# Reordering the queues of a cross-attention stage: scores behind the query product, normalises in one run, a subtraction ahead of the statistics

## The chip, the cores and the metric

The kernel runs on one core of a Trainium2 chip. Times are device microseconds of one execution. The engines are TensorE (PE, with its weight loads PEld), VectorE (DVE), ScalarE (ACT), GpSimd (POOL) and SyncE (SP), which here only issues transfers.

## The reference, cut to what matters

Six layers run one after the other on x (128 batches of 32 rows of 128). The change touches the first, a cross-attention of 16 heads with 64 features each. Its queries are the layer-normed rows of x ("latents"); its keys and values come from 257 context rows and the 32 latents.

```python
xn, ln_lat = layer_norm(ctx, g1, b1), layer_norm(latents, g2, b2)
q = ln_lat @ Wq
k, v = split(concatenate([xn, ln_lat], axis=1) @ Wkv)
weight = einsum('bhld,bhnd->bhln', q * scale, k * scale)
weight = softmax(where(full_mask, weight, neg), axis=-1)
out = einsum('bhln,bhnd->bhld', weight, v)
return out @ Wout                     # added to x
```

## The kernel before, in words

`xattn0` never forms keys and values. For each head it keeps the 128 x 128 products A (of the query and key weights) and U (of the value and output weights). So the scores are (latents x A) against the normed context rows, and the output is (probabilities x context rows) x U, summed over heads.

The work is cut into 128 batches. Four batches make a tile of 128 query rows, and 32 tiles make x. The 512 rows of a batch (16 heads x 32 rows) are worked on in four groups of 128. Each engine runs a function `step(g, j)` for batch s = 8g + j; the middle of the stage is a hardware loop over g with eight steps written out. Within a step the order of work on each engine is the order in the code, and semaphores order the engines among themselves. Different parts of a step serve different batches: `live(g, j, n)` says that batch s + n exists, so the edges of the stage leave parts out.

In a step for batch s TensorE does, in this order:

- `score` for groups 0 and 1 of batch s + 1 (L812), into two PSUM banks that the groups share by turns
- `turn` of batch s: eight transpositions of the normalised probabilities (L822)
- `score` for groups 2 and 3 of batch s + 1
- `query`: a quarter of the queries of the next tile (L859), into one PSUM bank
- in the first step of a tile (b == 0) the projection of the finished tile with U, 16 products (L881)
- the values of batch s in two halves (L840), and between them the transposition of the tails (L831) and of a context block of batch s + 3 (L893)
- the values of the tail rows (L851), with which the output of the batch is complete.

VectorE masks each group and takes its row extreme (L684), copies the first turned half (L695), takes statistics and normalises context rows for batches s + 4 and s + 5 (L703, L710, L717), forms the reciprocal of the four row sums (L722) and the scaled tail probabilities (L724), subtracts to get the low half of the queries (L731) and of the turned context (L740), and adds the projection to x (L736).

ScalarE takes the exponentials (L755), normalises each group of probabilities with the reciprocal (L760, four instructions a step), and copies out of PSUM: the second turned half (L769), the high half of the queries (L776), the turned tails (L785), the high half of the context (L791), and the output (L796).

A tile's score needs both halves of the queries, the turn of batch s + 1 needs all four normalises of it, and the tail values (L851) need the copy L785. GpSimd applies the affine part of the context norm, and SP loads context rows eight batches ahead, once z of the batch that used the slot is done.

Of the kernel before, what the change touches and what calls it, by code (L numbers as in the profile page):

```python
# [20 lines left out]
ALU = mybir.AluOpType  # L21
# [3 lines left out]
ds = bass.ds  # L25
# [414 lines left out]
def live(g, j, ahead, n=B):  # L440

    return not isinstance(g, int) or 0 <= 8 * g + j + ahead < n
# [93 lines left out]
def xattn0(k, io):  # L536
# [8 lines left out]
    with ExitStack() as stack:  # L545
# [42 lines left out]
        def quarter(b):  # L588


            return (1, b + 1) if b < 3 else (2, 0)
# [6 lines left out]
        with nc.Block() as block:  # L598
# [78 lines left out]
            @block.vector  # L677
            def _(dve):
                def mask(g, j, grp):
                    s, n, par = g * 8 + j, (j + 1) % 8, (j + 1) % 2  # L680
                    if n % 4 == 0 and grp == 0:
                        dve.wait_ge(keys_ready, tile_of(g, j, 1) + 1)
                    wait_apart(k, dve, scored, s * 4 + (5 + grp))
                    nc.vector.tensor_tensor_reduce(  # L684
                        out=neg[:, grp, :], in0=score_ps[grp % 2][:, 0:KEYS0], in1=bias[:, n, :], scale=-DH0 ** -0.5,
                        scalar=3.4e38, op0=ALU.add, op1=ALU.min, accum_out=nmax[:, par, grp:grp + 1]).then_inc(masked, 1)

                def step(g, j):
                    s, t, u, b = g * 8 + j, tile_of(g, j), j // 4, j % 4
                    if live(g, j, 1):  # L690
                        mask(g, j, 0)
                        mask(g, j, 1)
                    if live(g, j, 0):
                        dve.wait_ge(turned[0], s + 1)
                        nc.vector.tensor_copy(probT[:, 0, :], turn_ps[0][:]).then_inc(probT_ready[0], 1)  # L695
                    if live(g, j, 1):
                        mask(g, j, 2)
                        mask(g, j, 3)
                    if live(g, j, 5):
                        n, par = (j + 5) % 8, (j + 5) % 2  # L700
                        dve.wait_ge(raw_loaded[n], (g + (j + 5) // 8 + 1) * 16)
                        for kt in range(2):
                            last = nc.vector.bn_stats(stats[:, par, kt, :], raw[:, n, kt, :])  # L703
                        last.then_inc(stats_ready, 1)
                    if live(g, j, 4):
                        n, par = (j + 4) % 8, j % 2
                        dve.wait_ge(rstd_ready, s + 5)
                        wait(dve, xn_ready, s + 3)
                        for kt in range(2):
                            last = nc.vector.tensor_scalar(z[:, par, kt, :], raw[:, n, kt, :], mv[:, par, kt, 0:1],  # L710
                                                           rstd[:, par, kt:kt + 1], ALU.subtract, ALU.mult)
                        last.then_inc(z_ready, 1)
                    if live(g, j, 5):
                        par = (j + 5) % 2
                        wait_apart(k, dve, stats_ready, s + 6)
                        for kt in range(2):
                            last = nc.vector.bn_aggr(mv[:, par, kt, :], stats[:, par, kt, :])  # L717
                        last.then_inc(mv_ready, 1)
                    if live(g, j, 1):
                        par = (j + 1) % 2  # L720
                        dve.wait_ge(exped, s * 4 + 8)
                        nc.vector.reciprocal(rinv[:, par, :], rsum[:, par, :]).then_inc(rinv_ready, 1)  # L722
                        dve.wait_ge(rinv_ready, s + 2)
                        nc.vector.tensor_tensor(  # L724
                            prob_tail[:, par, :, :, 0:TAIL0].rearrange("p i f n -> p f i n"),
                            prob[:, par, :, 2 * P:KEYS0].rearrange("p (f i) n -> p f i n", f=2),
                            rinv[:, par, :].rearrange("p (f i) -> p f i", f=2).unsqueeze(3).broadcast_to([P, 2, 2, TAIL0]),
                            ALU.mult).then_inc(tail_prob_ready, 1)
                    if live(g, j, 4 * quarter(b)[0] - b):
                        dve.wait_ge(q_hi, (t + quarter(b)[0]) * 4 + (quarter(b)[1] + 1))  # L730
                        nc.vector.tensor_tensor(q_half(g, j, LO), q_ps[:].rearrange("p (h b l) -> p h b l", h=4, l=L),  # L731
                                                q_half(g, j, HI), ALU.subtract).then_inc(q_copied, 1)
                    if b == 0 and live(g, j, -1):
                        dve.wait_ge(proj_ready, t)
                        xt = k.x[:, ds((t - 1) * D, D)]
                        nc.vector.tensor_tensor(xt, proj_ps, xt, ALU.add).then_inc(x_added, 1)  # L736
                    if live(g, j, 3):
                        dve.wait_ge(xnT_hi, s + 4)
                        n = (j + 3) % 8
                        nc.vector.tensor_tensor(xnT[:, LO, n, 0:2 * P], ctx_ps[:, 0:2 * P], xnT[:, HI, n, 0:2 * P],  # L740
                                                ALU.subtract).then_inc(xnT_ready, 1)
                    if b == 0 and live(g, j, -1):
                        wait_apart(k, dve, x_added, t)
                        tile_stats(k, t - 1).then_inc(x_stats_ready, 1)

                dve.wait_ge(zeroed, 1)
                run_steps(dve, step, LEAD, LAG)
                dve.wait_ge(x_stats_ready, TILES)

            @block.scalar  # L750
            def _(act):
# [3 lines left out]
                    nc.scalar.activation(prob[:, par, grp, :], neg[:, grp, :], ACT.Exp, bias=nmax[:, par, grp:grp + 1],  # L755
                                         scale=-1.0, accum_out=rsum[:, par, grp:grp + 1]).then_inc(exped, 1)

                def normalise(g, j, grp):
                    part = prob[:, (j + 1) % 2, grp, 0:2 * P]
                    return nc.scalar.activation(part, part, ACT.Copy, scale=rinv[:, (j + 1) % 2, grp:grp + 1])  # L760

                def step(g, j):
                    s, t, u, b = g * 8 + j, tile_of(g, j), j // 4, j % 4
                    if live(g, j, 1):
# [2 lines left out]
                    if live(g, j, 0):  # L767
                        act.wait_ge(turned[1], s + 1)
                        nc.scalar.activation(probT[:, 1, :], turn_ps[1][:], ACT.Copy).then_inc(probT_ready[1], 1)  # L769
                    if live(g, j, 1):  # L770
                        exp(g, j, 2)
                        exp(g, j, 3)
                    ahead, hg = quarter(b)
                    if live(g, j, 4 * ahead - b):
                        act.wait_ge(q_ready, (t + ahead) * 4 + (hg + 1))
                        nc.scalar.activation(q_half(g, j, HI), q_ps[:].rearrange("p (h b l) -> p h b l", h=4, l=L),  # L776
                                             ACT.Copy).then_inc(q_hi, 1)
                    if live(g, j, 1):
                        act.wait_ge(rinv_ready, s + 2)
                        act.wait_ge(exped, s * 4 + 8)  # L780
                        normalise(g, j, 0)
                        normalise(g, j, 1)
                    if live(g, j, 0):
                        act.wait_ge(turned[2], s + 1)
                        nc.scalar.activation(probT[:, 2, 0:2 * P], turn_ps[0][:, 0:2 * P], ACT.Copy).then_inc(probT_ready[2], 1)  # L785
                    if live(g, j, 1):
                        normalise(g, j, 2)
                        normalise(g, j, 3).then_inc(prob_ready, 1)
                    if live(g, j, 3):
                        act.wait_ge(ctx_turned, s + 4)  # L790
                        nc.scalar.activation(xnT[:, HI, (j + 3) % 8, 0:2 * P], ctx_ps[:, 0:2 * P], ACT.Copy).then_inc(xnT_hi, 1)  # L791
                    if live(g, j, 0):
                        act.wait_ge(out_ready, s + 1)
                        if b == 0:
                            wait(act, proj_ready, t)
                        nc.scalar.activation(oT[:, :, b * L:(b + 1) * L].rearrange("p (f h) l -> p f h l", f=2),  # L796
                                             out_ps[:, :, 0:2 * P].rearrange("p f (h l) -> p f h l", l=L), ACT.Copy).then_inc(oT_ready, 1)
# [4 lines left out]
            def _(pe):  # L802
# [60 lines left out]
                def step(g, j):  # L863
# [5 lines left out]
                    if here:  # L869
                        turn(g, j, 0)  # L870
                        turn(g, j, 1)
                    if ahead:
                        score(g, j, 2)
                        score(g, j, 3)
                    if live(g, j, 4 * quarter(b)[0] - b):
                        query(g, j)
                    if b == 0 and live(g, j, -1):
                        pe.wait_ge(oT_ready, s)
                        wait(pe, xnT_ready, s + 3 if live(g, j, 2) else B)
                        for h in range(H):  # L880
                            last = nc.tensor.matmul(proj_ps, oT[:, h, :], k.U[:, h, :], start=(h == 0), stop=(h == H - 1))  # L881
                        last.then_inc(proj_ready, 1)
                    if here:
                        values(g, j, 0)
                        turn_tails(g, j)
# [1599 lines left out]
```

## Time and profile before

| | |
|---|---|
| median of 3 runs | 2382.99 us (2381.13 to 2385.65) |
| the profiled execution | 2381.13 us, of which its span is 2379.0 us |
| busy share of TensorE / weight loads | 84% / 65% |
| busy share of VectorE / ScalarE / GpSimd | 69% / 68% / 38% |
| granted TensorE clock, mean | 0.917 of full speed |

The stage that the change touches begins some 70 us after the span's start and ends at about 1030 us. A busy share is the time with at least one instruction in progress. TensorE's instructions are pipelined and their ends are modelled, so their starts are the better thing to read. VectorE's and ScalarE's instructions overlap their successors by a few hundredths of a microsecond.

### The profile page before, as it was taken

To read this page: it belongs to the slowest core of one execution; us is meant where nothing else is said; L and a number is where in the kernel's file an instruction comes from. 1 tells how busy PE (TensorE), PEld (TensorE's weight loads), DVE (VectorE), ACT (ScalarE), POOL (GpSimd) and SP (SyncE) were. 2 spreads that over 40 slices of the span, in tenths; PEclk is the share of its full clock that TensorE was granted. 3 is DMA by queue.
4 is the path that set the end of the run, shared out by engine and by line. 5 is a ranking of instruction groups with operands and counts; after the bars stand their busy time and mean duration, and the time that the engine had idled before them with its cause. 6 is when DMAs were issued, how large, how long until landed. Compare 5 with 4: busy or idle time off the path is not lost. (4 is left out here: it accounts for less than half of the span.)

```text
span 2379.0 us, 56007 instructions
## 1 busy us (share of the span) xinstructions
PE 1989.1 (84%) x15622; PEld 1552.4 (65%) x15622; DVE 1637.6 (69%) x5167; ACT 1626.3 (68%) x4429; POOL 907.8 (38%) x1342
## 2 busy tenths in 40 slices
PE   3799999999999999962600579999999989859997
PEld 2688888888888888841500247777777756526665
DVE  5777777777777777638667637787787778854554
ACT  3588888888777888852644358887887878644443
POOL 2533443334433333203145023333333357534554
PEclk8799999999999999985755789999999999969999
DMA  4211111111111111000000022222222100010001
GB/s 132 69 32 32 32 32 32 34 33 33 37 33 31 31 31 31 3 1 0 0 0 0 0 69 65 70 61 64 70 61 64 49 2 0 1 27 1 1 0 35
DMA packets 113673, 77.03 MB, mean 32 GB/s; under 512 B 12385, under 2 KB 99777, under 8 KB 113473
## 3 DMA queue, kind: packets, MB, share of 16 engines
q1 hardware_dynamic: 112086, 73.99, 11.5%
q10 hardware_dynamic: 1194, 1.58, 0.2%
q8 instruction: 34, 0.56, 0.1%
q0 software_dynamic: 320, 0.60, 0.1%
q14 instruction: 39, 0.31, 0.0%
HBM read 71.67 MB, written 4.46 MB: 32 GB/s over the span
## 5 line engine op out<-in xcount | busy, mean ns | idle before, releaser
L755 ACT ACTIVATE a_prob<-a_neg,a_nmax 128x289 f32<-128x289 f32 x512 | 270.4, 529 | 80.5 <-DVE a_nmax L684 75.0
L1646 ACT ACTIVATE b_prob<-b_neg,b_nmax 128x257 f32<-128x257 f32 x512 | 255.6, 505 | 97.6 <-DVE b_nmax L1596 97.5
L650 POOL TENSOR_TENSOR a_xn<-a_z,g 128x256 f32<-128x256 f32 x128 | 93.3, 729 | 525.4 <-DVE a_z L710 525.4
L812 PE MATMUL a_score<-a_xnT,a_qT 128*128 128x290 f32 x1536 | 274.3, 314 | 1.1 <-DVE a_qT L731 1.1
L840 PE MATMUL a_out<-a_probT,a_xn 128*128 128x256 f32 x1024 | 263.5, 380 | 0.3 <-DVE a_probT L695 0.3
L684 DVE CUSTOM_DVE_ANT_0 a_neg<-a_score,a_bias 128x289 f32<-128x289 f32 x512 | 220.9, 459 | 46.9 <-PE a_score L812 40.9
L812 PEld LDWEIGHTS a_score<-a_xnT,a_qT 128*128 128x128 f32 x1536 | 215.9, 190 | 43.8 <-issue 43.2
L760 ACT ACTIVATE a_prob<-a_prob,a_rinv 128x256 f32<-128x256 f32 x512 | 230.2, 498 | 1.0 <-DVE a_rinv L722 1.0
L1596 DVE CUSTOM_DVE_ANT_0 b_neg<-b_score,b_bias 128x257 f32<-128x257 f32 x512 | 195.9, 421 | 31.9 <-PE b_score L1688 31.8
L840 PEld LDWEIGHTS a_out<-a_probT,a_xn 128*128 128x128 f32 x1024 | 174.9, 191 | 13.7 <-DVE a_probT L695 0.6
L740 DVE TENSOR_TENSOR a_xnT<-a_ctx,a_xnT 128x256 fp32r<-128x256 f32 x128 | 54.4, 425 | 160.2 <-ACT a_xnT L791 160.2
L2348 POOL TENSOR_TENSOR m_hidden<-m_full,m_hidden 128x512 fp32r<-128x512 f32 (+1 forms) x88 | 113.9, 1294 | 128.7 <-ACT m_hidden L2329 128.7
L1574 POOL TENSOR_TENSOR b_weight<-own_value,b_rinv 128x128 f32<-128x128 f32 x128 | 51.3, 401 | 262.0 <-DVE b_rinv L1614 261.9
L859 PE MATMUL a_q<-latT,A 128*128 (+1 forms) x1024 | 139.6, 281 | 6.5 <-DVE a_qT L731 4.2
L1693 PE MATMUL b_turn<-ident,b_prob 128*128 128x128 f32 x1024 | 143.3, 281 | 0.0
L1693 PEld LDWEIGHTS b_turn<-ident,b_prob 128*128 128x128 f32 x1024 | 109.1, 141 | 46.3 <-ACT b_prob L1646 42.0
L859 PEld LDWEIGHTS a_q<-latT,A 128*128 128x128 f32 x1024 | 131.2, 197 | 7.9 <-DVE a_qT L731 5.2
L1390 PE MATMUL f_down<-f_up,f_downT 128*128 x48 | 23.3, 638 | 133.4 <-DVE f_up L1362 133.3
L822 PE MATMUL a_turn<-ident,a_prob 128*128 128x128 f32 x1024 | 132.7, 273 | 1.4 <-ACT a_prob L760 1.3
L2324 ACT ACTIVATE m_silu<-m_g 128x512 f32<-128x512 f32 (+1 forms) x88 | 52.6, 598 | 116.5 <-PE m_g L1986 116.5
L881 PE MATMUL a_ctx<-U,a_oT 128*128 128x128 f32 x1024 | 119.7, 275 | 0.7 <-ACT a_oT L796 0.7
L822 PEld LDWEIGHTS a_turn<-ident,a_prob 128*128 128x128 f32 x1024 | 118.8, 141 | 2.0 <-ACT a_prob L760 2.0
(472 smaller groups left out, 5321.1 us busy)
## 6 DMA issues: line engine op xcount, KB each, us to landing
a_raw<-in_ctx SPq DMA_DIRECT2D x128, 128.0 KB, 3.3
b_raw<-in_ctx SPq DMA_DIRECT2D x128, 128.0 KB, 3.2
a_kept<-keep SPq DMA_DIRECT2D x32, 257.0 KB, 3.9
b_kept<-keep SPq DMA_DIRECT2D x32, 257.0 KB, 3.6
b_v_rows<-ctx_tail_values SPq DMA_DIRECT2D x32, 256.0 KB, 3.5
a_tail<-latents_normalised SPq DMA_DIRECT2D x64, 64.0 KB
latents_normalised<-lat_affine SPq DMA_DIRECT2D x8, 256.0 KB, 2.3
out<-x SPq DMA_DIRECT2D x1, 2048.0 KB
```

Source lines behind the costliest of these rows:

```text
L684: nc.vector.tensor_tensor_reduce(out=neg[:, grp, :], in0=score_ps[grp % 2][:, 0:KEYS0], in1=bias[:, n, :], scale=-DH0 ** -0.5, scalar=3.4e ...
L755: nc.scalar.activation(prob[:, par, grp, :], neg[:, grp, :], ACT.Exp, bias=nmax[:, par, grp:grp + 1], scale=-1.0, accum_out=rsum[:, par, g ...
L760: return nc.scalar.activation(part, part, ACT.Copy, scale=rinv[:, (j + 1) % 2, grp:grp + 1])
L812: last = nc.tensor.matmul(score_ps[grp % 2][:, 0:even(KEYS0)], qT[:, a, un, bn, 4 * grp:4 * grp + 4, :], xnT[:, c, n, :], start=(p == 0), ...
L822: last = nc.tensor.transpose(turn_ps[kt][:, grp * P:(grp + 1) * P], prob[:, j % 2, grp, kt * P:(kt + 1) * P], k.ident[:])
L840: nc.tensor.matmul(out_ps[:, half, 0:2 * P], xn[:, j, kt, :], probT[:, kt, half * 2 * P:(half + 1) * 2 * P], start=(kt == 0), stop=False)
L859: last = nc.tensor.matmul(q_ps[:, h * P:(h + 1) * P], k.A[:, 4 * hg + h, :], k.latT[:, ds((t + ahead) * P, P)], start=True, stop=True)
L881: last = nc.tensor.matmul(proj_ps, oT[:, h, :], k.U[:, h, :], start=(h == 0), stop=(h == H - 1))
L1596: nc.vector.tensor_tensor_reduce(out=neg[:, par, grp, :], in0=score_ps[grp][:, 0:N_CTX], in1=bias[:, n, :], scale=-DH1 ** -0.5, scalar=3.4 ...
L1646: nc.scalar.activation(prob[:, n, grp, :], neg[:, par, grp, :], ACT.Exp, bias=nmax[:, par, grp:grp + 1], scale=-1.0, accum_out=rsum[:, n, ...
L1693: last = nc.tensor.transpose(turn_ps[kt][:, grp * P:(grp + 1) * P], prob[:, j % 4, grp, kt * P:(kt + 1) * P], k.ident[:])
L2348: nc.gpsimd.tensor_tensor(h[0:r1, LO, :], full[0:r1, 1 - u, :], h[0:r1, HI, :], ALU.subtract).then_inc(lo_ready, 1)
```

## The change

On three engines the order of a step is changed. No instruction, transfer or wait is added or removed.

- TensorE: scores of groups 2 and 3 go behind the query product and behind the projection.
- ScalarE: the exponentials of groups 2 and 3 go behind the copy of the queries; the four normalises, so far in two pairs around the copy of the tails, stand together behind the copy of the tails and the copy of the context.
- VectorE: the addition to x goes from near the step's end to ahead of the masks of groups 2 and 3; the subtraction for the queries goes from behind the reciprocal and the tail probabilities to directly behind those masks.

```diff
 # VectorE
                         nc.vector.tensor_copy(probT[:, 0, :], turn_ps[0][:]).then_inc(probT_ready[0], 1)
+                    if b == 0 and live(g, j, -1):
+                        dve.wait_ge(proj_ready, t)
+                        xt = k.x[:, ds((t - 1) * D, D)]
+                        nc.vector.tensor_tensor(xt, proj_ps, xt, ALU.add).then_inc(x_added, 1)
                     if live(g, j, 1):
                         mask(g, j, 2)
                         mask(g, j, 3)
+                    if live(g, j, 4 * quarter(b)[0] - b):
+                        dve.wait_ge(q_hi, (t + quarter(b)[0]) * 4 + (quarter(b)[1] + 1))
+                        nc.vector.tensor_tensor(q_half(g, j, LO), q_ps[:].rearrange("p (h b l) -> p h b l", h=4, l=L),
+                                                q_half(g, j, HI), ALU.subtract).then_inc(q_copied, 1)
                     if live(g, j, 5):
...
-                    if live(g, j, 4 * quarter(b)[0] - b):
-                        dve.wait_ge(q_hi, (t + quarter(b)[0]) * 4 + (quarter(b)[1] + 1))
-                        nc.vector.tensor_tensor(q_half(g, j, LO), q_ps[:].rearrange("p (h b l) -> p h b l", h=4, l=L),
-                                                q_half(g, j, HI), ALU.subtract).then_inc(q_copied, 1)
-                    if b == 0 and live(g, j, -1):
-                        dve.wait_ge(proj_ready, t)
-                        xt = k.x[:, ds((t - 1) * D, D)]
-                        nc.vector.tensor_tensor(xt, proj_ps, xt, ALU.add).then_inc(x_added, 1)
 # ScalarE
-                    if live(g, j, 1):
-                        exp(g, j, 2)
-                        exp(g, j, 3)
                     ahead, hg = quarter(b)
                     if live(g, j, 4 * ahead - b):
                         act.wait_ge(q_ready, (t + ahead) * 4 + (hg + 1))
                         nc.scalar.activation(q_half(g, j, HI), q_ps[:].rearrange("p (h b l) -> p h b l", h=4, l=L),
                                              ACT.Copy).then_inc(q_hi, 1)
                     if live(g, j, 1):
-                        act.wait_ge(rinv_ready, s + 2)
-                        act.wait_ge(exped, s * 4 + 8)
-                        normalise(g, j, 0)
-                        normalise(g, j, 1)
+                        exp(g, j, 2)
+                        exp(g, j, 3)
                     if live(g, j, 0):
                         act.wait_ge(turned[2], s + 1)
                         nc.scalar.activation(probT[:, 2, 0:2 * P], turn_ps[0][:, 0:2 * P], ACT.Copy).then_inc(probT_ready[2], 1)
-                    if live(g, j, 1):
-                        normalise(g, j, 2)
-                        normalise(g, j, 3).then_inc(prob_ready, 1)
                     if live(g, j, 3):
                         act.wait_ge(ctx_turned, s + 4)
                         nc.scalar.activation(xnT[:, HI, (j + 3) % 8, 0:2 * P], ctx_ps[:, 0:2 * P], ACT.Copy).then_inc(xnT_hi, 1)
+                    if live(g, j, 1):
+                        par = (j + 1) % 2
+                        act.wait_ge(rinv_ready, s + 2)
+                        act.wait_ge(exped, s * 4 + 8)
+                        for grp in range(GROUPS):
+                            last = nc.scalar.activation(prob[:, par, grp, 0:2 * P], prob[:, par, grp, 0:2 * P], ACT.Copy,
+                                                        scale=rinv[:, par, grp:grp + 1])
+                        last.then_inc(prob_ready, 1)
 # TensorE
-                    if ahead:
-                        score(g, j, 2)
-                        score(g, j, 3)
                     if live(g, j, 4 * quarter(b)[0] - b):
                         query(g, j)
                     if b == 0 and live(g, j, -1):
...
                         last.then_inc(proj_ready, 1)
+                    if ahead:
+                        score(g, j, 2)
+                        score(g, j, 3)
                     if here:
                         values(g, j, 0)
```

## Rows read from the trace of the kernel before

**Rows 1.** The page: the span, and each engine's busy time and share

```profile
span 2379.0 us, 56007 instructions
PE 1989.1 (84%) x15622; PEld 1552.4 (65%) x15622; DVE 1637.6 (69%) x5167; ACT 1626.3 (68%) x4429; POOL 907.8 (38%) x1342
```

**Rows 2.** Windows: this stage, the second attention stage, this stage's start

```profile
core 0: us, PE busy (x) PEld busy (x) DVE busy (x) ACT busy (x) POOL busy (x), PEclk, DMA share, GB/s
...
500.00:900.00 400.00, 399.44 (x2842) 349.62 (x2841) 289.07 (x1060) 322.57 (x924) 159.25 (x303) 1.00 0.12 32
1700.00:1900.00 200.00, 190.23 (x2106) 141.51 (x2099) 159.61 (x628) 161.67 (x557) 71.14 (x148) 1.00 0.24 62
75.00:80.00 5.00, 2.80 (x11) 2.51 (x12) 2.97 (x12) 0.60 (x1) 4.28 (x10) 0.50 0.71 203
```

**Rows 3.** Timeline of TensorE: start, duration, line, count; a projection, then regular steps

```profile
504.75 3.74 PE L881 MATMUL a_ctx<-U,a_oT 128*128 128x128 f32 x32
508.32 1.03 PE L840 MATMUL a_out<-a_probT,a_xn 128*128 128x256 f32 x4
...
511.21 1.07 PE L812 MATMUL a_score<-a_xnT,a_qT 128*128 128x290 f32 x6
512.12 1.03 PE L822 MATMUL a_turn<-ident,a_prob 128*128 128x128 f32 x8
512.91 1.05 PE L812 MATMUL a_score<-a_xnT,a_qT 128*128 128x290 f32 x6
513.80 1.05 PE L859 MATMUL a_q<-latT,A 128*128 x8
514.69 1.03 PE L840 MATMUL a_out<-a_probT,a_xn 128*128 128x256 f32 x4
...
516.00 1.03 PE L840 MATMUL a_out<-a_probT,a_xn 128*128 128x256 f32 x4
517.00 0.70 PE L851 MATMUL a_out<-a_probT,a_tail 64*128 64x256 f32 x4
517.63 1.07 PE L812 MATMUL a_score<-a_xnT,a_qT 128*128 128x290 f32 x6
...
531.43 0.82 PE L822 MATMUL a_turn<-ident,a_prob 128*128 128x128 f32 x6
```

**Rows 4.** Timeline of weight loads: tail values, with a projection and in a regular step

```profile
510.58 0.30 PEld L851 LDWEIGHTS a_out<-a_probT,a_tail 64*128 64x128 f32 x4 [0.33 <-issue]
...
517.00 0.30 PEld L851 LDWEIGHTS a_out<-a_probT,a_tail 64*128 64x128 f32 x4 [0.38 <-ACT a_probT L785]
```

**Rows 5.** Timeline of VectorE in the same regular step

```profile
513.75 0.46 DVE L684 CUSTOM_DVE_ANT_0 a_neg<-a_score,a_bias 128x289 f32<-128x289 f32 x1 [0.20 <-PE a_score L812]
...
514.15 0.46 DVE L684 CUSTOM_DVE_ANT_0 a_neg<-a_score,a_bias 128x289 f32<-128x289 f32 x1
...
515.59 0.14 DVE L722 RECIPROCAL a_rinv<-a_rsum 128x4 f32<-128x4 f32 x1
...
516.40 0.68 DVE L731 TENSOR_TENSOR a_qT<-a_q,a_qT 128x512 fp32r<-128x512 f32 x1
```

**Rows 6.** Timeline of ScalarE in the same regular step

```profile
514.78 0.52 ACT L755 ACTIVATE a_prob<-a_neg,a_nmax 128x289 f32<-128x289 f32 x1
...
515.78 0.90 ACT L760 ACTIVATE a_prob<-a_prob,a_rinv 128x256 f32<-128x256 f32 x2
516.59 0.36 ACT L785 ACTIVATE a_probT<-a_turn 128x256 f32<-128x256 f32 x1
516.85 0.90 ACT L760 ACTIVATE a_prob<-a_prob,a_rinv 128x256 f32<-128x256 f32 x2
```

**Rows 7.** Timeline of ScalarE and weight loads around the first turn

```profile
92.04 1.69 ACT L760 ACTIVATE a_prob<-a_prob,a_rinv 128x256 f32<-128x256 f32 x4
...
93.78 0.86 PEld L822 LDWEIGHTS a_turn<-ident,a_prob 128*128 128x128 f32 x8 [1.50 <-ACT a_prob L760]
```

**Rows 8.** Timeline of TensorE at the stage's end, one of three such waits

```profile
1020.52 0.70 PE L851 MATMUL a_out<-a_probT,a_tail 64*128 64x256 f32 x4 [0.96 <-ACT a_probT L785]
```

More of the change, by code:

```diff
@@ L756, in exp @@
                                          scale=-1.0, accum_out=rsum[:, par, grp:grp + 1]).then_inc(exped, 1)
-                def normalise(g, j, grp):
-                    part = prob[:, (j + 1) % 2, grp, 0:2 * P]
-                    return nc.scalar.activation(part, part, ACT.Copy, scale=rinv[:, (j + 1) % 2, grp:grp + 1])
                 def step(g, j):
```

## The prediction

> **What bounds the kernel now.** I read the page first: TensorE (PE) has the largest busy share, 84%, ahead of VectorE and ScalarE [rows 1]. All edits lie in `xattn0`, so I asked for windows. In the middle of that stage TensorE is busy 399.4 of 400 us at a granted clock of 1.00, while VectorE and ScalarE have 289 and 323 us of work [rows 2]. A busy TensorE can still be waiting between two groups, so the third view is the timeline, where I read starts and not ends. From one turn group (L822) to the third one after it are 531.43 - 512.12 = 19.31 us, 6.44 us a step [rows 3]. The groups of a step take, by their starts: scores 0, 1: 0.91; turn: 0.79; scores 2, 3: 0.89; query: 0.89; values, tail turn, context turn: 1.31 together; second values: 1.00; tail values 0.63. That is 6.42. So today TensorE's own work sets the period. The one wait left is before the tail values: 0.38 us of idle weight loading, put down to ScalarE's copy of the tail (L785) [rows 4]. In the step with the projection the same loads stand idle for 0.33 us without waiting for another engine, so this wait costs 0.05 us.
>
> The question is then how much room the dependency round has that TensorE's work now covers. The round is: turn of batch s, scores of s+1, masking on VectorE, exponentials on ScalarE, reciprocal on VectorE (L722), normalising on ScalarE (L760), turn of s+1. In one step: the turn begins at 512.12, scores 2, 3 at 512.91, the fourth mask at 514.15, the reciprocal at 515.59, the first normalise at 515.78, and the last pair starts at 516.85 and lasts 0.90, to 517.75 [rows 3, 5, 6]. A turn that did wait, the first of the stage, began 0.05 us after four normalises of 1.69 us ended (93.78 - 92.04 - 1.69) [rows 7]. The round thus takes 517.75 - 512.12 + 0.05 = 5.68 us, and its room under TensorE's 6.44 is 0.76 us. An edit that lengthens it by more moves the bound from TensorE to this round.
>
> **The change part by part.** It adds and removes no instruction, no transfer and no wait; it moves them on three queues.
>
> *TensorE.* Scores 2, 3 go behind the query and, in the first step of a tile, behind the projection. The query is a 0.89 us slot [rows 3], so the round becomes 0.89 longer. The projection (3.57 us from 504.75 to 508.32) now lies inside the round and not beside it; but it is TensorE's own time in either order, so a tile's first step is again the regular step plus 3.57.
>
> *ScalarE.* The tail copy (L785) and the context copy (L791) come before the normalises, and the four normalises are one run. The tail copy used to stand inside the run: its 0.26 us (516.59 to 516.85) leaves the round, and the run of four takes 1.69 [rows 6, 7]. The copies now fill time in which ScalarE would wait for the reciprocal: the fourth exponential starts 0.63 us behind its mask and lasts 0.52 [rows 5, 6], and two copies at 0.26 each are through 1.7 us behind the mask, while the reciprocal in the new order lets the first normalise go 2.2 us behind it. They are costed at nothing, under that cover; without it they would cost 0.5 a step. The query copy (L776) moves ahead of exponentials 2 and 3, which have to wait for later scores anyway, so it is free too. Queued behind the late normalises are the output copy (L796) and the next exponentials: the output copy is first needed by the projection, 1.68 us behind the turn, and ScalarE has 323 of 400 us of work [rows 2].
>
> *VectorE.* The subtraction that makes the low half of the queries (L731) goes from behind the reciprocal to directly behind the fourth mask, ahead of the statistics, z, aggregation and the reciprocal. From fourth mask to reciprocal VectorE runs without a gap, 1.44 us (514.15 to 515.59). So the reciprocal comes a whole subtraction later. It lasts 0.68; neighbours overlap by 0.06 (a mask lasts 0.46, its successor starts 0.40 later) [rows 5], so I take 0.62. Bounds: 0.40, the pitch of the shorter rows, and 0.68, no overlap. The addition into x (L736) moves ahead of masks 2 and 3. It waits for the projection, which now stands ahead of scores 2, 3; it has a quarter of the columns of L731's 0.68 us, and even 0.68 would fit in the 0.84 us from the start of scores 2 (512.91) to their mask (513.75). It costs nothing, and what is queued behind it is waiting for the same engine. POOL's work and SP's loads hang on z, later by 1.5 us; the loads are issued eight batches ahead.
>
> *The sum for a regular step*, from turn to turn: turn and query 0.79 + 0.89, and 0.02 more since a burst after a wait starts cold (0.91 against 0.89 for scores); scores 2, 3 to fourth mask 1.24; mask to reciprocal 1.44 + 0.62; reciprocal to normalise 0.19; four normalises 1.69; to the turn 0.05. Together 6.93 us against 6.44: 0.49 more. The same by differences: 0.89 + 0.62 - 0.26 = 1.25, less 0.76 of room, leaves 0.49. TensorE alone would need 6.38 to 6.40, so it now stands still for half a microsecond in front of each turn.
>
> *How often.* 128 batches; the last tile has no queries, so the round of batches 0 to 122 is affected: 123 x 0.49 = 60 us. At the stage's start TensorE has the lower clock [rows 2], and scores 2, 3 go behind a query of twice 0.89: about 2 us more, once. At its end, where no query follows, three steps wait up to 0.96 us for the tail copy [rows 8]; it now comes before the normalises, and about 3 us come back. Net +59.
>
> The profiled execution took 2381.1 us (span 2379.0, 2.1 around it), 1.9 below the median of three runs. 2381.1 + 59 = 2440 for its like, 2442 for the median.
>
> **The granted clock.** TensorE would now stand still for about 7% of each step. Rows first: in the later attention stage it is busy 190.2 of 200 us and holds 1.00; where it is busy about half the time it is at 0.50, which is 1.2 against 2.4 GHz [rows 2]. So I expect 1.00. The Trainium skill, page "TensorE: Matmul & The Clock Gate", section "A second HAM failure mode: psum-queue depth-cycling", tells of a kernel whose short pauses between groups were enough to make the clock go up and down. By that rule the loss would be larger than my sum, and it is rival D below; the row of the later stage speaks against it.
>
> **The rivals.**
>
> B, no change: the round still fits under TensorE's work. For it: TensorE is at 99.9% in the window and gets no more work. It would need the reciprocal not to be pushed by the subtraction; without that 0.62 the round is 6.31, under 6.40, and the time stays within 2 to 3 us of 2383. Against it: VectorE runs gap-free from mask to reciprocal. The Trainium skill, page "Perfetto Trace Analysis", section "Identifying the Most-Contended Engine", has one look for the engine with the highest occupancy, for TensorE that of its weight loads. Here it is TensorE too, with 349.6 of 400 us, its work is unchanged, and taken alone that gives this rival. 6%.
>
> C, faster: the tail copy ahead of the normalises removes the only wait TensorE has, 0.05 us in each of 96 regular steps, 5 us, and 3 us at the end of the stage: 2375. It decides only if the round is below 6.40, the same point as in B, and if the start costs nothing. 4%.
>
> D, slower still: the pauses lower the clock. At 0.50 TensorE's 6.4 us become 12.8, 5.9 us more than 6.93 for each such step; a tenth of the steps, 13, gives another 75 us, about 2517. 6%.
>
> A, the forecast: 84%, of which some lies outside its own range of sizes.
>
> **How the numbers follow.** The likeliest is A, 2442. Its size: a subtraction of 0.40 gives 0.27 a step (+32 us in all, 2415), one of 0.68 gives 0.55 (+67, 2450). Engines that start after a wait may add up to 0.05 at each of four handoffs, 0.2 a step, +25: 2467 from the middle and 2475 from the top. Both ends together are unlikely; I take 2420 to 2468. B, C and D are outside, 16 in 100, and a few in 100 of A. This kernel can be told from no change from about 0.2% on, 5 us: faster 0.04 (C), same 0.06 (B), slower 0.90 (A and D).
>
> **What would show it.** In the trace after: regular turns 6.9 us apart and those over a projection 10.5; the turn (L822) waiting about 0.5 us for a normalise, about 120 times, where today nothing waits; the fourth mask followed by the subtraction, the reciprocal 2.06 us behind the mask and not 1.44; ScalarE idle in front of the normalises, released by the reciprocal; no wait of the tail values for the tail copy; later stages as before. I am wrong if the reciprocal comes with the exponentials' end rather than VectorE's, if turns stay 6.44 apart, or if the clock in this stage is under 1.00.

## The result, and the profile after

The changed kernel takes 2450.6 us, median of four runs (2449.74 to 2452.95), beside 2382.9 us for the kernel before: ratio 1.0285, 95% interval 1.0267 to 1.0303. It is slower by 68 us; 2442 was forecast. In rows of the changed kernel the turn is L818, scores L808, the query L855, the projection L874, the subtraction L705, the reciprocal L730, the tail copy L776, the context copy L779 and the normalises L785.

The page: span and engines, beside [rows 1].

```profile
span 2447.2 us, 56021 instructions
PE 2013.7 (82%) x15622; PEld 1552.1 (63%) x15622; DVE 1633.9 (67%) x5167; ACT 1632.6 (67%) x4429; POOL 906.6 (37%) x1342
```

Each engine runs as many instructions as before, over a longer span. Windows in the two attention stages, beside [rows 2]:

```profile
500.00:900.00 400.00, 380.94 (x2649) 324.71 (x2649) 268.36 (x989) 303.99 (x863) 148.37 (x282) 1.00 0.11 30
1760.00:1960.00 200.00, 189.73 (x2090) 141.01 (x2088) 160.62 (x629) 161.23 (x555) 72.20 (x149) 1.00 0.24 62
```

Only the first changed: TensorE is no longer full, and its clock still is. Its timeline, beside [rows 3]:

```profile
520.15 1.09 PE L818 MATMUL a_turn<-ident,a_prob 128*128 128x128 f32 x8 [0.37 <-ACT a_prob L785]
521.08 1.06 PE L855 MATMUL a_q<-latT,A 128*128 x8
521.89 1.05 PE L808 MATMUL a_score<-a_xnT,a_qT 128*128 128x290 f32 x6
...
527.12 1.09 PE L818 MATMUL a_turn<-ident,a_prob 128*128 128x128 f32 x8 [0.37 <-ACT a_prob L785]
...
534.10 1.09 PE L818 MATMUL a_turn<-ident,a_prob 128*128 128x128 f32 x8 [0.36 <-ACT a_prob L785]
...
544.64 1.09 PE L818 MATMUL a_turn<-ident,a_prob 128*128 128x128 f32 x8 [0.37 <-ACT a_prob L785]
```

A regular step takes 6.97 us (520.15 to 527.12), the one with a projection 10.54, which is 3.57 more. Each turn waits for a normalise. Weight loads, beside [rows 4], show this wait as 0.61 us, and the tail values without the extra 0.05 they had:

```profile
525.04 0.30 PEld L847 LDWEIGHTS a_out<-a_probT,a_tail 64*128 64x128 f32 x4 [0.33 <-ACT a_probT L776]
...
527.12 0.86 PEld L818 LDWEIGHTS a_turn<-ident,a_prob 128*128 128x128 f32 x8 [0.61 <-ACT a_prob L785]
```

VectorE, beside [rows 5]: fourth mask, subtraction, reciprocal.

```profile
523.14 0.46 DVE L684 CUSTOM_DVE_ANT_0 a_neg<-a_score,a_bias 128x289 f32<-128x289 f32 x1
...
523.52 0.69 DVE L705 TENSOR_TENSOR a_qT<-a_q,a_qT 128x512 fp32r<-128x512 f32 x1
...
525.17 0.15 DVE L730 RECIPROCAL a_rinv<-a_rsum 128x4 f32<-128x4 f32 x1
```

ScalarE, beside [rows 6] and [rows 7]: the two copies, then 0.43 us of waiting for the reciprocal, then the run of four.

```profile
524.30 0.36 ACT L776 ACTIVATE a_probT<-a_turn 128x256 f32<-128x256 f32 x1
524.56 0.37 ACT L779 ACTIVATE a_xnT<-a_ctx 128x256 fp32r<-128x256 f32 x1
525.36 1.71 ACT L785 ACTIVATE a_prob<-a_prob,a_rinv 128x256 f32<-128x256 f32 x4 [0.43 <-DVE a_rinv L730]
```

Who waited for whom between 80 and 1060 us (total us, times, longest):

```profile
PEld a_turn L818 <- ACT a_prob L785: 78.2, 123, 3.0
```

123 turns wait, and two more between 1060 us and the end of the stage. In the same view of the kernel before, whose stage lies within it, two turns wait, 2.0 us in all. At the stage's end the waits of [rows 8] are gone, but one turn waits 0.85 us:

```profile
1087.33 1.09 PE L818 MATMUL a_turn<-ident,a_prob 128*128 128x128 f32 x8 [0.85 <-ACT a_prob L785]
```

### The profile page after: what moved, and what is told of

Its sections match the earlier page's. It is cut to its first block and busy times, and to the rows that moved or that the text cites. A ratio compares the mean times of both kernels' runs of the same rounds, so it can differ in the third digit from the quotient of the medians.

```text
span 2447.2 us, 56021 instructions
## 1 busy us (share of the span) xinstructions
PE 2013.7 (82%) x15622; PEld 1552.1 (63%) x15622; DVE 1633.9 (67%) x5167; ACT 1632.6 (67%) x4429; POOL 906.6 (37%) x1342
## 5 line engine op out<-in xcount | busy, mean ns | idle before, releaser
L808 PE MATMUL a_score<-a_xnT,a_qT 128*128 128x290 f32 x1536 | 273.9, 314 | 0.4 <-DVE a_qT L705 0.4
L785 ACT ACTIVATE a_prob<-a_prob,a_rinv 128x256 f32<-128x256 f32 x512 | 218.6, 498 | 55.2 <-DVE a_rinv L730 55.2
L808 PEld LDWEIGHTS a_score<-a_xnT,a_qT 128*128 128x128 f32 x1536 | 216.2, 190 | 42.7 <-issue 41.9
L818 PE MATMUL a_turn<-ident,a_prob 128*128 128x128 f32 x1024 | 140.7, 281 | 50.4 <-ACT a_prob L785 50.4
L818 PEld LDWEIGHTS a_turn<-ident,a_prob 128*128 128x128 f32 x1024 | 110.4, 141 | 80.4 <-ACT a_prob L785 80.2
L855 PE MATMUL a_q<-latT,A 128*128 (+1 forms) x1024 | 140.8, 282 | 5.3 <-DVE a_qT L705 2.9
L855 PEld LDWEIGHTS a_q<-latT,A 128*128 128x128 f32 x1024 | 129.2, 198 | 6.6 <-DVE a_qT L705 4.0
L695 DVE COPY a_probT<-a_turn 128x512 f32<-128x512 f32 x128 | 88.5, 692 | 54.6 <-PE a_turn L818 54.6
L874 PE MATMUL a_ctx<-U,a_oT 128*128 128x128 f32 x1024 | 119.7, 275 | 0.7 <-ACT a_oT L792 0.7
```

What stands on the lines that cost most here:

```text
L785: last = nc.scalar.activation(prob[:, par, grp, 0:2 * P], prob[:, par, grp, 0:2 * P], ACT.Copy, scale=rinv[:, par, grp:grp + 1])
L808: last = nc.tensor.matmul(score_ps[grp % 2][:, 0:even(KEYS0)], qT[:, a, un, bn, 4 * grp:4 * grp + 4, :], xnT[:, c, n, :], start=(p == 0), ...
L818: last = nc.tensor.transpose(turn_ps[kt][:, grp * P:(grp + 1) * P], prob[:, j % 2, grp, kt * P:(kt + 1) * P], k.ident[:])
L855: last = nc.tensor.matmul(q_ps[:, h * P:(h + 1) * P], k.A[:, 4 * hg + h, :], k.latT[:, ds((t + ahead) * P, P)], start=True, stop=True)
```

## The experiments

All ten compute the whole reference. "Step" is the distance of two turns without a projection between them. Each ratio is to executions of the kernel before that were timed beside the run, with medians of 2382.9 to 2384.0 us.

| run | what is changed | median us | ratio to before (95%) | step us |
|---|---|---|---|---|
| changed kernel | | 2450.6 | 1.0285 (1.0267 to 1.0303) | 6.97 |
| e1 | after, subtraction back | 2397.6 | 1.0057 (1.0041 to 1.0072) | 6.42, once a tile 6.95 |
| e10 | after, subtraction behind the reciprocal | 2379.1 | 0.9984 (0.9974 to 0.9994) | 6.41 |
| e7 | after, scores 2, 3 ahead of the projection | 2430.4 | 1.0197 (1.0177 to 1.0216) | 6.9 to 7.1 |
| e6 | after, addition into x back | 2529.4 | 1.0612 (1.0594 to 1.0630) | 6.9 to 7.1 |
| e9 | after, normalises in two pairs | 2571.8 | 1.0786 (1.0768 to 1.0804) | 7.92 |
| e12 | after, copy of the queries back | 2650.3 | 1.1117 (1.1098 to 1.1136) | 8.34 and more |
| e4 | before, normalises in one run | 2372.9 | 0.9955 (0.9941 to 0.9968) | 6.38 |
| e3 | before, scores moved | 2560.0 | 1.0737 (1.0721 to 1.0753) | 7.34 |
| e11 | before, scores and addition moved | 2495.2 | 1.0475 (1.0457 to 1.0492) | 7.32 |
| e2 | before, subtraction moved | 2683.5 | 1.1260 (1.1243 to 1.1277) | 8.4 and more |

**e1: the subtraction back where it was.**

```diff
 # VectorE, in the changed kernel
                         mask(g, j, 3)
-                    if live(g, j, 4 * quarter(b)[0] - b):
-                        ... q_half(g, j, LO) = q_ps - q_half(g, j, HI)
...
                             ALU.mult).then_inc(tail_prob_ready, 1)
+                    if live(g, j, 4 * quarter(b)[0] - b):
+                        ... q_half(g, j, LO) = q_ps - q_half(g, j, HI)
```

> The changed kernel with VectorE's query subtraction back behind the reciprocal and the tail probabilities. Theory (the dependency round from turn to turn binds at 6.97 us, and the subtraction lies in it): the round loses 0.6 us, falls to 6.36 and lies under TensorE's own 6.40; about 2378 to 2383 us, the whole loss gone, and no turn waits for a normalise. Rival (the later scores alone make the loss, the subtraction is hidden behind the exponentials): near 2450. Rival (ScalarE's new order makes it): near 2450.

53 of the 68 us go, and of the 128 turns only the first and the last still wait for a normalise. The rest is a new wait, once a tile: its first scores (in the step b = 3) need the subtraction of the step before.

```profile
529.34 1.07 PE L808 MATMUL a_score<-a_xnT,a_qT 128*128 128x290 f32 x6 [0.48 <-DVE a_qT L735]
```

0.48 us in 31 tiles are 15 us, and 2397.6 - 15 = 2383. So the round was the cause, and the size of this run's expectation was missed by a wait that I had not looked for.

**e2: only the subtraction moved, in the kernel before.**

```diff
 # VectorE, in the kernel before
                         mask(g, j, 3)
+                    if live(g, j, 4 * quarter(b)[0] - b):
+                        ... q_half(g, j, LO) = q_ps - q_half(g, j, HI)
...
-                    if live(g, j, 4 * quarter(b)[0] - b):
-                        ... q_half(g, j, LO) = q_ps - q_half(g, j, HI)
```

> The kernel before with nothing but VectorE's query subtraction directly behind the fourth mask. Theory: the round grows from 5.68 to 6.30 us and stays under TensorE's 6.44; 2383 us, within 5 us. Rival (the subtraction costs by itself whatever the order of TensorE): 0.6 us in each of 123 steps, near 2455.

Both expectations failed: the loss is 300 us. VectorE's timeline in this run:

```profile
503.93 0.46 DVE L684 CUSTOM_DVE_ANT_0 a_neg<-a_score,a_bias 128x289 f32<-128x289 f32 x1
...
505.66 0.69 DVE L701 TENSOR_TENSOR a_qT<-a_q,a_qT 128x512 fp32r<-128x512 f32 x1 [1.26 <-ACT a_qT L776]
...
507.32 0.14 DVE L726 RECIPROCAL a_rinv<-a_rsum 128x4 f32<-128x4 f32 x1
```

TensorE's in and behind the same step:

```profile
500.34 0.70 PE L851 MATMUL a_out<-a_probT,a_tail 64*128 64x256 f32 x4 [1.96 <-ACT a_probT L785]
...
508.72 0.82 PE L851 MATMUL a_out<-a_probT,a_tail 64*128 64x256 f32 x4 [1.95 <-ACT a_probT L785]
509.47 1.82 PE L812 MATMUL a_score<-a_xnT,a_qT 128*128 128x290 f32 x6
```

And a window, with the columns of [rows 2]:

```profile
500.00:900.00 400.00, 339.66 (x2133) 300.03 (x2134) 225.90 (x800) 255.06 (x703) 119.03 (x227) 0.90 0.09 23
```

The subtraction waits 1.26 us for ScalarE's copy of the queries (L776), which in this kernel stands behind the exponentials of the masks just finished. The reciprocal is queued behind it, and ScalarE's tail copy behind the reciprocal. TensorE then stands still for about 1.95 us in a step without a projection, and its clock falls: six score products that span 1.07 us at the full clock span 1.82. In a step with a projection it does not wait. TensorE's waits for the tail copy over the whole stage, 80 to 1345 us (total us, times, longest):

```profile
PE a_out L851 <- ACT a_probT L785: 182.2, 96, 2.1
```

The pauses are thus some 180 of the 300 us. By difference, 96 steps of 8.38 (500.34 to 508.72) and not 6.44 us are 186, and about 110 us are left, in which the products ran slower: 73 of the 128 turns span over 1.2 us, and 1.03 is their span at the full clock.

**e3: only the scores moved, in the kernel before.**

```diff
 # TensorE, in the kernel before
-                    if ahead:
-                        score(g, j, 2)
-                        score(g, j, 3)
                     if live(g, j, 4 * quarter(b)[0] - b):
                         query(g, j)
                     if b == 0 and live(g, j, -1):
...
+                    if ahead:
+                        score(g, j, 2)
+                        score(g, j, 3)
                     if here:
                         values(g, j, 0)
```

> The kernel before with nothing but scores 2 and 3 moved behind the query and the projection on TensorE. Theory: the round is 1.74 (turn, query) + 1.25 + 1.44 + 0.19 + 1.97 (normalises with the tail copy between) + 0.05 = 6.64 us against 6.44, so 0.2 in 123 steps, +25 us: 2408, turns waiting 0.2 to 0.3 us for the normalise. Rival (the score move alone makes the loss): near 2450. Rival (it is hidden, only the subtraction counts): 2383.

Missed again: 177 us and not 25. Who waited for whom, 500 to 900 us (total us, times, longest):

```profile
PE a_out L851 <- ACT a_probT L785: 31.4, 35, 1.0
...
PE a_ctx L893 <- DVE x L736: 26.2, 11, 2.4
```

No turn waits. The waits are in places that the one round I had drawn does not pass. The first is a second round: tail values, scores 0 and 1, turn, scores 2 and 3, fourth mask, reciprocal, first pair of normalises, tail copy, tail values. In the kernel before, with [rows 3], [rows 5] and [rows 6], it is 0.63 + 0.91 + 0.79 + 1.24 + 1.44 + 0.19 + 0.81 + 0.41 = 6.42 us. That is the step of 6.44 to within 0.02, so this round had no room, where the first had 0.76. The query's 0.89 in it gives 7.3, and 7.34 was measured. It also gives the step of e2, where the reciprocal comes 3.39 us behind the fourth mask (503.93 to 507.32) and not 1.44: 6.42 + 1.95 = 8.37, with 8.38 measured. The second wait is the context turn's, 2.4 us in each step with a projection, for the addition into x.

**e11: scores and addition moved.** As e3, and on VectorE the addition (`dve.wait_ge(proj_ready, t)` and the line it guards) goes ahead of `mask(g, j, 2)`.

> The kernel before with two moves: scores 2, 3 behind the query and the projection on TensorE, and the addition into x ahead of masks 2, 3 on VectorE. Theory of the second round (the one through the tail copy): the score move alone costs 7.33 - 6.44 = 0.89 us in 123 steps, 109 us, and the other 68 us of the run with the score move alone came from the context turn that waited 2.4 us for the addition in each of 31 projection steps; with the addition ahead that part is gone: 2384 + 109 = 2493. Rival (the 2.4 us are owed to something else in those steps): 2560, as in that run.

2495.2: the two parts are 112 us for the second round and 65 us for the addition. The list of waits, from which the context turn's is gone:

```profile
PE a_out L851 <- ACT a_probT L785: 43.5, 49, 1.0
```

**e4: only the normalises in one run, in the kernel before.**

```diff
 # ScalarE, in the kernel before
-                        normalise(g, j, 0)
-                        normalise(g, j, 1)
                     if live(g, j, 0):
                         ... tail copy
-                    if live(g, j, 1):
-                        normalise(g, j, 2)
-                        normalise(g, j, 3).then_inc(prob_ready, 1)
                     if live(g, j, 3):
                         ... context copy
+                    if live(g, j, 1):
+                        ... wait for the reciprocal and the exponentials
+                        ... normalise 0, 1, 2, 3
```

> The kernel before with ScalarE's four normalises in one run behind the tail copy and the context copy, nothing else. Theory: TensorE stays the bound (the run ends 0.1 us before the turn is due), its only wait, 0.05 us before the tail values, goes, and so do three waits of 0.7 to 1.0 us at the end of the stage: 2375, 2373 to 2380. Rival (ScalarE's new order costs, because the normalises now wait for TensorE's context turn): slower than 2383, up to 0.3 us a step, 2420.

2372.9, the fastest version of all. TensorE has no wait left, and a turn follows every 6.38 us:

```profile
514.48 1.04 PE L821 MATMUL a_turn<-ident,a_prob 128*128 128x128 f32 x8
...
520.86 1.03 PE L821 MATMUL a_turn<-ident,a_prob 128*128 128x128 f32 x8
```

The window:

```profile
500.00:900.00 400.00, 400.00 (x2859) 352.38 (x2859) 287.90 (x1071) 327.77 (x932) 157.58 (x299) 1.00 0.12 32
```

**e9: the normalises in two pairs around the tail copy, in the changed kernel** (the reverse of e4's diff).

> The changed kernel with ScalarE's normalises again in two pairs around the tail copy, and the context copy behind them. Theory of the second round (reciprocal, first pair, tail copy, tail values on TensorE, next scores, turn, query, scores 2, 3, fourth mask, reciprocal): 0.63 + 0.91 + 1.70 + 1.25 + 2.03 + 0.19 + 0.81 + 0.41 = 7.93 us a step, 0.96 more than the changed kernel in 123 steps: 2450 + 118 = 2568, the wait before the tail values about 1.5 us, no wait before the turn. Rival (the prediction's view, only the round through all four normalises counts, the tail copy in it costs 0.26): 2450 + 32 = 2482.

2571.8, as the second round has it; the turns no longer wait, the tail values do.

```profile
510.07 0.70 PE L851 MATMUL a_out<-a_probT,a_tail 64*128 64x256 f32 x4 [1.47 <-ACT a_probT L783]
...
511.62 1.03 PE L822 MATMUL a_turn<-ident,a_prob 128*128 128x128 f32 x8
```

The window, in which the clock stays full:

```profile
500.00:900.00 400.00, 331.69 (x2347) 288.68 (x2346) 239.81 (x886) 272.44 (x772) 131.91 (x250) 1.00 0.10 25
```

**e6: the addition into x back, in the changed kernel** (VectorE, again behind the tail probabilities).

> The changed kernel with VectorE's addition into x back near the step's end. TensorE's context turn waits for this addition in the step with the projection. Theory of the second run set (each move on one queue needs its partner on another): the addition stands behind mask, subtraction, statistics, reciprocal and tail probabilities and ends about 4.2 us after the start of scores 2, 3, where the context turn is due after 2.0; so TensorE is 2.2 late, of which 0.4 to 0.5 is swallowed by the wait it has anyway: 1.7 us in each of 31 such steps, 2450 + 53 = 2503. Rival (what the prediction said, the move of the addition costs and gains nothing): 2450.

The mechanism is as expected, the cost 79 us and not 53:

```profile
530.48 1.09 PE L818 MATMUL a_turn<-ident,a_prob 128*128 128x128 f32 x8 [0.37 <-ACT a_prob L785]
...
540.31 0.41 PE L889 MATMUL a_ctx<-ident,a_xn 128*128 128x128 f32 x2 [2.38 <-DVE x L736]
...
543.07 1.03 PE L818 MATMUL a_turn<-ident,a_prob 128*128 128x128 f32 x8
```

The step takes 12.59, 2.05 more than 10.54, which is 64 us in 31. The other 15 us lie with the clock, 0.98 between 500 and 900 us: 11 of the 31 steps with a projection take 14.0 to 14.2 us, because the products behind the pause span up to 1.88 us and not 1.03. In one of them:

```profile
675.80 0.41 PE L889 MATMUL a_ctx<-ident,a_xn 128*128 128x128 f32 x2 [2.38 <-DVE x L736]
676.05 1.88 PE L836 MATMUL a_out<-a_probT,a_xn 128*128 128x256 f32 x4
```

**e7: scores 2, 3 behind the query but ahead of the projection, and the addition back.** In the diff of e3 the added lines stand above `if b == 0 and live(g, j, -1)`.

> The changed kernel with scores 2, 3 behind the query but ahead of the projection, and the addition into x back where it was. Theory: the dependency round then runs beside the projection and not after it, so the step with the projection is bound by TensorE's own work, 10.0 us and not 10.54, the others stay at 6.97: 31 x 0.5 = 16 us less than the changed kernel, 2434. Rival (the projection lies beside nothing either way): 2450.

2430.4. The step with the projection falls from 10.54 to 10.01, and its turn does not wait:

```profile
526.80 1.09 PE L818 MATMUL a_turn<-ident,a_prob 128*128 128x128 f32 x8 [0.36 <-ACT a_prob L785]
...
536.81 1.03 PE L818 MATMUL a_turn<-ident,a_prob 128*128 128x128 f32 x8
```

The addition stands at its old, late place here too, and no context turn waits for it. So its early place is needed only where scores 2, 3 stand behind the projection.

**e10: the subtraction directly behind the reciprocal, in the changed kernel.** As e1, but the lines go in ahead of the tail probabilities.

> The changed kernel with VectorE's query subtraction directly behind the reciprocal, ahead of the tail probabilities. Theory: the round is 6.97 - 0.62 = 6.35, under TensorE's 6.38, and the subtraction is 0.6 us earlier than in the run with the subtraction at its old place, so the scores of a new tile no longer wait 0.48 us for it: 2375 to 2380. Rival (a wait of another kind takes the place, as in that run): 2390 to 2398.

2379.1. With 0.62 us out of the round and the new tile's wait avoided, the whole loss is gone. TensorE is full again, at 6.41 a step:

```profile
517.55 1.08 PE L819 MATMUL a_turn<-ident,a_prob 128*128 128x128 f32 x8
...
523.96 1.07 PE L819 MATMUL a_turn<-ident,a_prob 128*128 128x128 f32 x8
```

**e12: the copy of the queries back behind exponentials 2 and 3, in the changed kernel** (ScalarE).

> The changed kernel with ScalarE's copy of the queries back behind exponentials 2 and 3. Theory: VectorE's subtraction, directly behind the fourth mask, then has to wait for this copy, which starts 0.63 + 0.53 us behind the mask and lasts 0.58: the reciprocal and with it the round come 1.4 us later, 8.37 us a step, 2450 + 172 = 2622, more if pauses of 1.9 us bring the clock down. Rival (the place of this copy is free, as the prediction said of it): 2450.

2650.3. The subtraction waits 1.29 us for the copy, and the turn 1.61. VectorE:

```profile
506.18 0.69 DVE L705 TENSOR_TENSOR a_qT<-a_q,a_qT 128x512 fp32r<-128x512 f32 x1 [1.29 <-ACT a_qT L772]
```

TensorE:

```profile
509.78 1.09 PE L818 MATMUL a_turn<-ident,a_prob 128*128 128x128 f32 x8 [1.61 <-ACT a_prob L785]
...
521.70 1.97 PE L818 MATMUL a_turn<-ident,a_prob 128*128 128x128 f32 x8 [1.61 <-ACT a_prob L785]
```

The second of these turns spans 1.97 us against 1.09. Of the 127 turns after the first of the stage, 19 span 1.5 us or more: behind some of these pauses the clock has gone to its lower level. It is 0.97 between 500 and 900 us.

## Why the prediction was right, step by step

**The round of a regular step.** 6.93 was summed, 6.97 measured. By terms: turn and query 1.74 (1.70 summed; the turn after a wait takes 0.93, the query then 0.81), scores to fourth mask 1.25 (1.24), mask to reciprocal 2.03 (2.06), reciprocal to normalise 0.19 (0.19), four normalises 1.71 (1.69), to the turn 0.05. The largest miss is the start of the turn after a wait.

**Its place as the bound.** Shown by e1 and e10: with the subtraction out of it the round is shorter than TensorE's work, and no turn waits. Rival B named this term as the one that decides, and e10 lies 4 us under the kernel before, where B had 2 to 3 us either way. This does not make the subtraction the only cause: by the same sum the round without the 0.89 us of the later scores would be about 6.1 us (6.97 less 0.89), under TensorE's work too. No run put only the scores back.

**The projection inside the round**, shown by the 10.54 and by e7. "It is TensorE's own time in either order" was right only as to the sum of TensorE's work: kept beside the round it gives 20 us back.

**The count and the edges.** The stage ends 66.0 us later, by the first transposition of the next one (1037.07 to 1103.08). The second turn comes 2.9 us later (100.68 to 103.61; 2 had been taken), 122 steps cost 0.53 each, 65 us, and the end returns 1.9 (3 taken). The remaining 2 us of span lie behind the stage and have no cause that I could find. The forecast was 59 us where 68 were measured: 5 from 0.53 against 0.49, 2 from the edges, 2 behind the stage.

**What was right for an incomplete reason.** The prediction gave ScalarE's copies and the addition into x no price and saw only one round. The whole change passes with that, and this was in part luck: it happens to contain the moves that make it so. e3, e9 and e11 show the second round, through the tail copy. It was what held the old order at 6.44, by little: the 0.05 us that the prediction read as a wait beside TensorE's own work, and with it gone e4 runs at 6.38. The tail copy's 0.26 us in the prediction were its part in the first round alone. e2 and e12 show that the early copy of the queries is what makes the early subtraction possible, and e3, e6 and e11 that, behind a projection, the early addition is what lets the context turn go on time. The changed kernel without one of its moves is slower by 121 us (e9, the normalises in one run), 200 (e12, the early copy of the queries) and 79 (e6, the early addition). For a smaller edit drawn from the same text the prediction would have been wrong, as my expectations for e2 and e3 were.

**Rival C.** Its mechanism is real, 2372.9 in e4 against 2375 forecast for it, as long as nothing else is moved. In the whole change the longer round covers it.

**Rival D and the clock.** The granted clock stayed at 1.00 with a pause of 0.37 us in each step, as the row of the later stage had it, and also in e9 with a pause of 1.47. It fell to 0.90 in e2, with pauses of 1.95, and over the same window was 0.97 in e12 (1.61), 0.98 in e6 (2.38, once a tile) and 0.99 in e3 (0.9, and 2.38 once a tile). What the Trainium skill, page "TensorE: Matmul & The Clock Gate", section "A second HAM failure mode: psum-queue depth-cycling", tells of one kernel, that short pauses make the clock go up and down, is thus seen in e2, now and then in e12, e6 and e3, and not in the changed kernel nor in e9.

## What to carry to other kernels

When the fullest engine sets the pace, draw every round of dependencies that passes through its queue, one for each instruction on it that waits for another engine, and sum each: the one with the least room decides what a reordering costs. An instruction moved forward on one queue brings its wait with it, so ask what its source stands behind on the other queue; such moves are good or bad as a set. And look at the parts of a set one by one afterwards: here one part of the change, alone, was 10.7 us faster than the kernel before.

## What the runs showed of the hardware that was not expected

A TensorE that pauses 1.47 us in every step of 7.9, busy 332 of 400 us, kept the full clock (e9). With pauses of 1.95 us in the steps without a projection it had 0.90 over the same window (e2), and score products and turns behind a pause went on at the lower level. Behind pauses of 1.61 us most turns ran at the full clock and some at the lower one (e12), and so did the products behind the pause of 2.38 us that e6 has once a tile: slower in 11 of 31. These pauses stand at different places of the step, so whether their length alone decides is not shown. So one extra wait on VectorE cost 300 us in e2: some 180 are TensorE's pauses, and about 110, by difference, the lower clock.
